# Attention block in fp32: maxima split and turned on VectorE, later q and k split on GpSimd

## The chip, the cores and the metric

The kernel runs on one core of a Trainium2 chip. The metric is device time in microseconds (us) of one execution, the median of several. Engines: TensorE (PE) for matrix products, VectorE (DVE), ScalarE (ACT), GpSimd (POOL), and SyncE (SP), which here only issues DMAs. They run side by side and meet at semaphores. Only PE writes products, to the memory PSUM; POOL and DMAs reach SBUF alone, not PSUM.

## What is computed

Eight batches of 512 rows of 128 numbers go through a layer norm with modulation, attention with 16 heads of 8 numbers, a gated sum, a second norm, and three dense layers with weights of +1 and -1. The attention, cut from the reference:

```python
pos = 1.0 + x * (1.0 + 0.5 * x * (1.0 + x / 3.0))
neg = 1.0 / (1.0 - x * (1.0 - 0.5 * x * (1.0 - x / 3.0)))
...
logits = logits - jnp.max(logits, axis=axis, keepdims=True)
s = _stablemax3_s(logits)
return s / jnp.sum(s, axis=axis, keepdims=True)
...
h = _layernorm(x, axis=-1) * (1 + ca) + sa
x = x + ga * _L0_attn_ref(h, L0_attn_w_qkv, L0_attn_w_out, L0_attn_b_out)
h = _layernorm(x, axis=-1) * (1 + cb) + sb
x = x + gb * _L0_ffn_ref(h, L0_ffn_k0, L0_ffn_k1, L0_ffn_k2, L0_ffn_s0, L0_ffn_s1, L0_ffn_s2)
```

After the maximum is taken off no logit is positive, so only the branch `neg` is used: one over a cubic.

## The kernel before, in words

The work is cut into 128 groups, 16 for each batch. A group m is two heads' worth of 512 x 256 scores, and belongs to a quad of four groups (`QUAD`). The program runs in steps s from -16 to 159; a block is 16 steps (b = s // 16, n = s % 16), and "step 5" below means n = 5. Every engine has its own function for a step (`pe_step`, `act_step`, `dve_step`, `pool_step`, `sp_step`), and each executes its instructions strictly in the order in which they are written there.

In step s the group s is finished and the logits of group s + 7 (`AHEAD`) are made, only for their row maxima:

- PE: `logits` writes the logits of two heads into the PSUM tensor SA (two banks, one for each head); `scores` writes scores, with the maximum taken off by two extra rows of the operand QH, into Z (two halves); `with_v` multiplies finished probabilities by v, five steps later; `misc` puts in pieces of the other layers at the places "a", "c" and "d" of the step, by the tables `MAIN` and `MISC`.
- ACT: `square_of` squares Z (L541), `prob_of` takes the reciprocal root of group s - 2 (L552), `take` copies products of the other layers out of PSUM.
- DVE: `cubic` (L701) twice and `maxima` (L712) twice, in turn. These four are the large DVE instructions. SA is a single buffer, so PE and DVE pass it to and fro.
- POOL: squares the cubic's result (L844), one instruction of 128x2048 per step, and norms (`normalise`, L850), gate products and copies.

A product in single precision is made of parts: a value is stored as a high part (rounded, type fp32r) and a low part (the rest). For q and k of the next batch, ACT writes the high part from PSUM (L568) and DVE the low part from PSUM (`split`, L734); SP writes both to memory (`write_parts`, L344) and reads them back spread over rows (`read_parts`, L348).

The maxima must go from a column for each row of q into rows of QH. Once in a quad, at n = 1, 5, 9 and 13: PE transposes the 128x16 maxima into SA's second bank (`maxima_across`, L484); DVE writes high and low part from there (`take_maxima`, L723 and L725); SP sends them to QH with four DMAs (L978). As the second bank of SA is taken for that time, the first logits of the next quad are made for each head alone (`alone`), and reduced in two instructions of 128x512. Behind these four DMAs SP issues the four that gather numerators and denominators of a finished quad (nd<-OT, L989). At n = 6 ACT squares the denominators of the whole batch (`den_sq`, L603), which needs all gathers.

MISC and AT say in which step and place the pieces of the other layers and of the norms stand; block 7 has no q, k and v to make, and blocks 8 and 9 hold what is left after the last group.

## Time and profile before

| | us |
|---|---|
| median of 3 runs | 790.41 (789.8 to 790.81) |
| the profiled execution | 786.48 |
| its span in the trace | 784.6 |
| steps 0 to 127 (47.4 to 724.6) | 677 |
| before the first cubic, after the last | 47, 60 |
| DVE busy in the span | 660.6 (84%) |
| PE, ACT, POOL busy | 654.2, 590.3, 584.9 |

Times in rows are microseconds from the start of the span, unless ns stands there. A name like mx<-SA is the tensor written and the one read. Idle time of an engine stands in brackets with the instruction that ended it. The clock of PE has two levels in this trace, 1.2 and 2.4 GHz: the column PEclk is its granted share, 1.00 for 2.4 GHz.

### The profile page before, as it was taken

To read this page: it belongs to the slowest core of one execution; us is meant where nothing else is said; L and a number is where in the kernel's file an instruction comes from. 1 tells how busy PE (TensorE), PEld (TensorE's weight loads), DVE (VectorE), ACT (ScalarE), POOL (GpSimd) and SP (SyncE) were. 2 spreads that over 40 slices of the span, in tenths; PEclk is the share of its full clock that TensorE was granted. 3 is DMA by queue.
4 is the path that set the end of the run, shared out by engine and by line. 5 is a ranking of instruction groups with operands and counts; after the bars stand their busy time and mean duration, and the time that the engine had idled before them with its cause. 6 is when DMAs were issued, how large, how long until landed. Compare 5 with 4: busy or idle time off the path is not lost.

```text
span 784.6 us, 9551 instructions
## 1 busy us (share of the span) xinstructions
PE 654.2 (83%) x2897; PEld 242.1 (31%) x2897; DVE 660.6 (84%) x806; ACT 590.3 (75%) x539; POOL 584.9 (75%) x348
## 2 busy tenths in 40 slices
...
DMA packets 41110, 56.35 MB, mean 72 GB/s; under 512 B 7852, under 2 KB 24516, under 8 KB 41060
## 3 DMA queue, kind: packets, MB, share of 16 engines
...
## 4 chain that ended last, share of the span: by engine, by line
PE 44%; DVE 24%; issue 15%; ACT 14%; DMA 1%; ACTq 0%; DVEq 0%; POOL 0%; POOLq 0%
DVE mx L712 12%; PE MB L417 10%; DVE cub L701 9%; PE OP L499 8%; PE SA L478 8%; PE Z L458 7%; ACT prob L552 5%; ACT sq L541 5%; PE MB L426 3%; PE SA L417 2%; PE MB L391 2%; ACT hid L582 2%; PE SA L426 1%; PE MB L394 1%; PE MB L410 1%
## 5 line engine op out<-in xcount | busy, mean ns | idle before, releaser
L844 POOL TENSOR_TENSOR cub<-cub 128x2048 f32<-128x2048 f32 x128 | 460.3, 3604 | 111.4 <-DVE cub L701 111.4
L541 ACT ACTIVATE sq<-Z,shift 128x1024 f32<-128x1024 f32 x256 | 282.9, 1117 | 110.9 <-PE Z L458 108.8
L712 DVE TENSOR_REDUCE mx<-SA 128x2 f32<-128x1024 f32 (+1 forms) x278 | 307.0, 1105 | 35.9 <-PE SA L478 34.6
L701 DVE SCALAR_TENSOR_TENSOR cub<-sq,Z 128x1024 f32<-128x1024 f32 x256 | 309.5, 1210 | 12.1 <-ACT sq L541 10.8
L552 ACT ACTIVATE prob<-cub 128x2048 f32<-128x2048 f32 x128 | 244.2, 1910 | 0.0
L478 PE MATMUL SA<-KH,QL 64*128 64x512 f32 x496 | 145.7, 523 | 62.3 <-DVE mx L712 51.4
L458 PE MATMUL Z<-QH,KH 64*128 64x512 f32 x512 | 139.8, 536 | 28.9 <-DVE cub L701 28.0
L499 PE MATMUL OP<-prob,Vq 128*16 128x512 f32 x1024 | 145.1, 641 | 1.4 <-ACT OT L590 1.4
L458 PEld LDWEIGHTS Z<-QH,KH 64*128 64x128 f32 x512 | 52.5, 199 | 222.3 <-DVE cub L701 145.7
L417 PE MATMUL MB<-hid,W 128*128 128x512 f32 x216 | 119.3, 640 | 0.0
L478 PEld LDWEIGHTS SA<-KH,QL 64*128 64x128 f32 x496 | 56.6, 200 | 162.0 <-DVE mx L712 132.1
L582 ACT ACTIVATE hid<-MB,sv 128x512 f32<-128x512 f32 x57 | 39.4, 691 | 9.1 <-PE MB L417 6.7
L410 PE MATMUL MB<-h2T,W 128*128 128x512 f32 x60 | 34.5, 658 | 9.5 <-ACT hid L582 7.8
L417 PEld LDWEIGHTS MB<-hid,W 128*128 128x128 f32 x216 | 32.9, 188 | 29.7 <-issue 28.8
L499 PEld LDWEIGHTS OP<-prob,Vq 128*16 128x16 f32 x1024 | 17.1, 95 | 38.6 <-issue 35.9
L426 PE MATMUL MB<-W2G,hid 128*128 128x128 f32 x192 | 27.3, 287 | 0.0
L753 DVE TENSOR_TENSOR y<-SA,x1k 128x512 f32<-128x512 f32 x2 | 1.4, 692 | 28.8 <-PE SA L426 28.8
L426 PEld LDWEIGHTS MB<-W2G,hid 128*128 128x128 f32 x192 | 23.1, 191 | 5.4 <-issue 5.4
L572 ACT ACTIVATE Vn<-MB 128x512 f32<-128x512 f32 x8 | 4.8, 600 | 24.4 <-PE MB L394 24.4
L814 POOL TENSOR_TENSOR rs<-mv,eps 128x4 f32<-128x4 f32 x16 | 3.3, 206 | 25.9 <-DVE mv L776 17.9
L850 POOL TENSOR_SCALAR x1n<-x,mv,rs 128x128 f32<-128x128 f32 x28 | 21.9, 800 | 0.7
L850 POOL TENSOR_SCALAR xn<-xa,mv,rs 128x128 f32<-128x128 f32 x28 | 21.9, 800 | 0.1
...
## 6 DMA issues: line engine op xcount, KB each, us to landing
...
nd<-OT SPq DMA_DIRECT2D x128, 32.0 KB
...
QH<-mp SPq DMA_DIRECT2D x128, 4.0 KB
```

The source lines that it names most:

```text
L417: mm = nc.tensor.matmul(bank, W1[:, kc, m * P:(m + 1) * P], hid[0][:, kc, :], start=(kc == 0), stop=(kc == KC - 1))
L426: mm = nc.tensor.matmul(bank4[:, t, :], hid[1][:, kc, t * P:(t + 1) * P], W2G[:, kc, :], start=(kc == 0), stop=(kc == KC - 1))
L458: mm = nc.tensor.matmul(Z[:, h, e * S:(e + 1) * S], KH[rows, 2 * g + r, keys], QH[rows, 2 * g + r, :], start=True, stop=True)
L478: nc.tensor.matmul(unit_bank(m, u)[:, e, :], QL[rows, 2 * g + r, qt * P:(qt + 1) * P], KH[rows, 2 * g + r, :], start=True, stop=True).then ...
L499: mm = nc.tensor.matmul(OP[32 * j:32 * j + 2 * HD, :], Vq[:, tb, hh, :, :].rearrange("p d a -> p (d a)"), slot[:, tb % 2, j % 2, :], start ...
L541: nc.scalar.activation(sq[:, h, :], Z[:, h, :], ACT.Square, bias=shift[:, 0:1]).then_inc(s_sq, 1)
L552: nc.scalar.activation(prob[:, m % RING, :], cub[:, m % RING].rearrange("p a n -> p (a n)"), RSQRT)\
L582: nc.scalar.activation(hid[layer][:, j, :], bank, ACT.Relu, scale=sv[:, layer:layer + 1])\
L701: nc.vector.scalar_tensor_tensor(cub[:, m % RING, h, :], sq[:, h, :], CUB_ADD, Z[:, h, :], ALU.add, ALU.mult).then_inc(s_cv, 1)
L712: nc.vector.tensor_reduce(to, unit_bank(m, u)[:, heads[0]:heads[-1] + 1, :], AX_X, ALU.max)\
L844: nc.gpsimd.tensor_tensor(ff, ff, ff, ALU.mult).then_inc(s_fp, 1)
L850: last = nc.gpsimd.tensor_scalar(dst[:, t, :], src[:, t, :], mv[:, t, 0:1], rs[:, t:t + 1], ALU.subtract, ALU.mult)
```

## The change

- The raw maxima (mx, 128x16 in SBUF) are first split into high and low part by DVE, in SBUF (`of_maxima`, stages 0 and 1), into ms (128x32); then DVE turns ms in blocks of 32x32 (stage 2, into mp). PE's transpose, its semaphore and `alone` are gone: the first logits of a quad are made and reduced like all others. The DMAs to QH are eight per quad (`M_DMAS`), one for each head and 32 partitions, in pieces of 128 bytes.
- From the second batch on, ACT copies q and k unsplit to SBUF, which frees the PSUM bank, and POOL makes both parts in SBUF (`parts_of`), at n = 1 and 2. SP waits for POOL's semaphores. k's product moves from place "d" of step 1 to "c", POOL's copy of v for quad 2 from step 1 to 3.
- `normalise` of POOL computes x * rs + nm with nm = -mean * rs in place of (x - mean) * rs; two instructions on 128x4 make nm.
- In the block ahead of the first group v is made at step 2. In block 7 x1, y and what follows move one step or a place ahead, and the second norm's statistics and root too; in block 8 l1_1 is cut into two halves (steps 0 and 1) and l1_2 is made in one piece in step 4.

```diff
-    ("hT", 1, [(0, "c", 4)]), ("q", 1, [(0, "d", 4)]), ("k", 1, [(1, "d", 4)]),
+    ("hT", 1, [(0, "c", 4)]), ("q", 1, [(0, "d", 4)]), ("k", 1, [(1, "c", 4)]),
...
+MISC[FIRST] = [("hT", 1, [(0, "c", 4)]), ("q", 1, [(0, "d", 4)]), ("k", 1, [(1, "d", 4)]), ("v", 1, [(2, "c", 4)])]
...
-    ("l1_1", -2, [(0, "c", 4)]), ("l1_2", -2, [(2, "c", 2), (4, "d", 2)]), ("l1_3", -2, [(5, "c", 4)]),
+    ("l1_1", -2, [(0, "c", 2), (1, "d", 2)]), ("l1_2", -2, [(4, "d", 4)]), ("l1_3", -2, [(5, "c", 4)]),
...
-AT[B - 1] = MAIN_AT | {"w2g": 4, "mv2": 9, "rs2": 10, "x1n": 10}
+AT[B - 1] = MAIN_AT | {"w2g": 4, "st2": 8, "mv2": 8, "rs2": 9, "x1n": 9}
...
-            def maxima_across(m):
-                if 0 <= m < GROUPS and m % QUAD == QUAD - 1:
-                    pe.wait_ge(s_mx, 4 * (m + 1))
-                    nc.tensor.transpose(SA[0:QUAD * TB, 1, 0:P], mx[:, m // QUAD % 2, :], ident[:, :]).then_inc(s_mt, 1)
...
-            if alone(m):
-                logits(m, 0, (1,))
             misc("a")
-            logits(m, 1, (0, 1))
+            logits(m, 1)
...
                             need(act, s_parts[name], beta * 4 * 16)
...
+                            if beta == 0:
+                                nc.scalar.activation(dst[:, 0, :], bank, ACT.Copy, scale=scale).then_inc(s_hi, 1)
+                            else:
+                                nc.scalar.activation(dst[:, 1, :].bitcast(F32), bank, ACT.Copy, scale=scale)\
+                                    .then_inc(s_taken[name], 1)
...
+                raw = mx[:, i, :].rearrange("p (e c) -> p e c", e=2)
+                if stage == 0:
+                    dve.wait_ge(s_mx, 2 * m)
+                    nc.vector.tensor_scalar(ms[:, i, :, 0, :], raw, -1.0, None, ALU.mult).then_inc(s_mh, 1)
+                elif stage == 1:
+                    dve.wait_ge(s_mh, quad + 1)
+                    nc.vector.scalar_tensor_tensor(ms[:, i, :, 1, :], raw, -1.0, ms[:, i, :, 0, :].bitcast(F32),
+                                                   ALU.mult, ALU.subtract).then_inc(s_ml, 1)
+                else:
+                    dve.wait_ge(s_ml, quad + 1)
+                    if quad >= 2:
+                        dve.wait_ge(s_mrow[(quad - 2) % NQ], ((quad - 2) // NQ + 1) * M_DMAS * 16)
+                    nc.vector.transpose(mp[:, i, :], ms[:, i].rearrange("p e a c -> p (e a c)").bitcast(F32))\
+                        .then_inc(s_mp, 1)
...
             cubic(s, 0)
-            take_maxima(m)
-            if alone(m):
-                maxima(m, 0, (0,))
-                maxima(m, 0, (1,))
-            else:
-                maxima(m, 0, (0, 1))
+            of_maxima(m, 0)
+            maxima(m, 0)
+            of_maxima(m, 1)
             split(b, n)
...
             cubic(s, 1)
-            maxima(m, 1, (0, 1))
+            of_maxima(m, 2)
+            maxima(m, 1)
...
+            def normalise(beta, k, src, mv, rs, nm, dst, s_rs, s_free, s_nm, s_done):
                 pool.wait_ge(s_rs, beta + 1)
+                nc.gpsimd.tensor_tensor(nm[:, :], mv[:, :, 0], rs[:, :], ALU.mult).then_inc(s_nm, 1)
+                pool.wait_ge(s_nm, 2 * k + 1)
+                nc.gpsimd.tensor_scalar(nm[:, :], nm[:, :], -1.0, 0.0, ALU.mult, ALU.add).then_inc(s_nm, 1)
+                pool.wait_ge(s_nm, 2 * k + 2)
                 need(pool, s_free, beta)
                 for t in range(TB):
-                    last = nc.gpsimd.tensor_scalar(dst[:, t, :], src[:, t, :], mv[:, t, 0:1], rs[:, t:t + 1],
-                                                   ALU.subtract, ALU.mult)
+                    last = nc.gpsimd.tensor_scalar(dst[:, t, :], src[:, t, :], rs[:, t:t + 1], nm[:, t:t + 1],
+                                                   ALU.mult, ALU.add)
...
+            def parts_of(beta, name):
+                if beta >= B:
+                    return
+                src = SQ if name == "q" else SK
+                i = 2 * beta + "qk".index(name)
+                pool.wait_ge(s_taken[name], beta + 1)
+                nc.gpsimd.tensor_scalar(src[:, 0, :], src[:, 1, :].bitcast(F32), 1.0, 0.0, ALU.mult, ALU.add)\
+                    .then_inc(s_hi, 1)
+                pool.wait_ge(s_hi, i + 1)
+                nc.gpsimd.tensor_tensor(src[:, 1, :], src[:, 1, :].bitcast(F32), src[:, 0, :].bitcast(F32), ALU.subtract)\
+                    .then_inc(s_lo, 1)
...
-            if n in (1, 5):
-                v_in(b, 2 if n == 1 else 3)
+            if n in (1, 2) and 0 <= b < B:
+                parts_of(b + 1, "qk"[n - 1])
+            if n in (3, 5):
+                v_in(b, 2 if n == 3 else 3)
...
                 for e in range(2):
-                    for a in range(PARTS):
-                        r = ROWS * e + R_MAX + a
-                        sp.dma_start(QH[r:r + 1, 2 * g:2 * g + 2, :].bitcast(F32), mp[2 * TB * e:2 * TB * (e + 1), quad % 2, a, :].bitcast(F32))\
+                    r = ROWS * e + R_MAX
+                    for k in range(P // 32):
+                        of = 32 * k + QUAD * TB * e
+                        sp.dma_start(rows_g[r:r + PARTS, :, :, k, :].bitcast(F32), mp[of:of + QUAD * TB, quad % 2, :])\
                             .then_inc(s_mrow[g], 16)
```

On DVE a step with a turn (n = 5 of block 0; the others are alike) is, before:

```order
L701 SCALAR_TENSOR_TENSOR cub<-sq,Z 128x1024
L723 TENSOR_SCALAR mp<-SA 16x128
L725 SCALAR_TENSOR_TENSOR mp<-SA,mp 16x128
L712 TENSOR_REDUCE mx<-SA 128x1 x2
L701 SCALAR_TENSOR_TENSOR cub<-sq,Z 128x1024
L712 TENSOR_REDUCE mx<-SA 128x2
```

and after:

```order
L699 SCALAR_TENSOR_TENSOR cub<-sq,Z 128x1024
L719 TENSOR_SCALAR ms<-mx 128x2x8
L708 TENSOR_REDUCE mx<-SA 128x2
L722 SCALAR_TENSOR_TENSOR ms<-mx,ms 128x2x8
L699 SCALAR_TENSOR_TENSOR cub<-sq,Z 128x1024
L728 STREAM_TRANSPOSE mp<-ms 128x32
L708 TENSOR_REDUCE mx<-SA 128x2
```

The two small instructions no longer stand together and no longer read SA; one stands on each side of the first reduction, which is whole again, and the transpose stands ahead of the second.

On SP the loads of a quad, the maxima (QH<-mp) and the gathers (nd<-OT) before:

```order
L348 DMA QL<-parts_q 32x1024 x2
L348 DMA KH<-parts_k 32x1024 x2
L348 DMA QH<-parts_q 32x1024 x2
L978 DMA QH<-mp 1x8x128 x4
L989 DMA nd<-OT 8x2x512 x4
```

and after:

```order
L354 DMA QL<-parts_q 32x1024 x2
L354 DMA KH<-parts_k 32x1024 x2
L354 DMA QH<-parts_q 32x1024 x2
L999 DMA QH<-mp 2x8x32 x8
L1010 DMA nd<-OT 8x2x512 x4
```

The order is the same; eight DMAs stand ahead of the gathers in place of four.

On POOL the steps 0 to 5 of a block (x1k is step 0's copy, cub<-cub a step's square), before:

```order
L865 TENSOR_SCALAR x1k<-x 128x512
L844 TENSOR_TENSOR cub<-cub 128x2048
L860 COPY Vq<-Vn 128x4x32
L844 TENSOR_TENSOR cub<-cub 128x2048 x4
L860 COPY Vq<-Vn 128x4x32
L873 TENSOR_TENSOR woG<-wo,gA 128x128
```

and after:

```order
L882 TENSOR_SCALAR x1k<-x 128x512
L845 TENSOR_TENSOR cub<-cub 128x2048
L865 TENSOR_SCALAR SQ<-SQ 128x512
L868 TENSOR_TENSOR SQ<-SQ 128x512
L845 TENSOR_TENSOR cub<-cub 128x2048
L865 TENSOR_SCALAR SK<-SK 128x512
L868 TENSOR_TENSOR SK<-SK 128x512
L845 TENSOR_TENSOR cub<-cub 128x2048
L877 COPY Vq<-Vn 128x4x32
L845 TENSOR_TENSOR cub<-cub 128x2048 x2
L877 COPY Vq<-Vn 128x4x32
L892 TENSOR_TENSOR woG<-wo,gA 128x128
```

The parts of q stand ahead of the square of step 1, those of k ahead of the square of step 2.

## Rows read from the trace of the kernel before

**Rows 1.** Windows: step 1 of block 1; block 3 and its steps 1, 2, 5, 9, 13.
```profile
core 0: us, PE busy (x) PEld busy (x) DVE busy (x) ACT busy (x) POOL busy (x), PEclk, DMA share, GB/s
136.35:145.58 9.23, 8.42 (x25) 2.73 (x25) 5.93 (x10) 5.75 (x6) 3.84 (x3) 0.50 0.07 17
306.16:391.76 85.60, 76.50 (x361) 27.70 (x361) 80.38 (x96) 73.30 (x68) 72.49 (x44) 1.00 0.27 81
311.20:318.54 7.34, 4.68 (x23) 1.52 (x21) 5.84 (x9) 5.90 (x7) 3.67 (x3) 1.00 0.05 13
318.54:324.38 5.84, 4.45 (x20) 1.47 (x20) 5.21 (x6) 4.40 (x5) 3.60 (x2) 1.00 0.81 297
333.71:339.71 6.00, 5.22 (x22) 1.66 (x22) 5.15 (x8) 4.40 (x5) 4.26 (x4) 1.00 0.03 8
354.64:361.19 6.55, 5.52 (x29) 2.23 (x28) 6.51 (x14) 5.47 (x6) 6.47 (x8) 1.00 0.04 9
375.38:382.06 6.68, 5.65 (x38) 3.22 (x38) 5.75 (x10) 4.69 (x5) 6.68 (x3) 1.00 0.04 11
```

**Rows 2.** Timeline of step 5, block 3: start us, us, engine line, what, [idle before].
```profile
332.74 3.60 POOL L844 TENSOR_TENSOR cub<-cub 128x2048 f32<-128x2048 f32 x1 [1.20 <-DVE cub L701]
333.71 1.21 DVE L701 SCALAR_TENSOR_TENSOR cub<-sq,Z 128x1024 f32<-128x1024 f32 x1
...
334.84 0.27 DVE L723 TENSOR_SCALAR mp<-SA 16x128 fp32r<-16x128 f32 x1
...
335.35 0.67 DVE L712 TENSOR_REDUCE mx<-SA 128x1 f32<-128x512 f32 x1
...
336.84 0.69 DVE L712 TENSOR_REDUCE mx<-SA 128x1 f32<-128x512 f32 x1 [0.82 <-PE SA L478]
...
338.58 1.22 DVE L712 TENSOR_REDUCE mx<-SA 128x2 f32<-128x1024 f32 x1
```

**Rows 3.** Groups by line: line engine op, shapes, count | busy us, mean ns | idle.
```profile
L850 POOL TENSOR_SCALAR xn<-xa,mv,rs 128x128 f32<-128x128 f32 x28 | 21.9, 800 | 0.1
...
L882 POOL TENSOR_TENSOR nd<-nd 128x512 f32<-128x512 f32 x7 | 8.9, 1276 | 14.0 <-ACT nd L596 14.0
...
L734 DVE SCALAR_TENSOR_TENSOR SQ<-MB,SQ 128x512 fp32r<-128x512 f32 x8 | 5.4, 680 | 0.9 <-ACT SQ L568 0.9
```

**Rows 4.** Timeline at start and end; L661 and L785: ns min/median/max.
```profile
5.32 1.03 POOL L816 TENSOR_TENSOR rs<-rs,half 128x4 f32<-128x4 f32 x1
...
5.99 0.28 DVE L637 TENSOR_TENSOR prob<-prob 8x128 f32<-8x128 f32 x1
...
9.26 1.90 POOL L832 TENSOR_SCALAR W<-prob 128x2048 f32<-128x2048 uint8 x1 [2.00 <-DMA prob<-L_ffn_k]
...
L661 DVE TENSOR_SCALAR mod<-mod x2: 158/580/1001, 10.2 to 11.1; 128x8 f32<-128x8 f32 x2
...
753.48 0.62 POOL L865 TENSOR_SCALAR x1k<-x 128x512 f32<-128x512 f32 x1 [1.61 <-DVE y L753]
...
L785 DVE TENSOR_SCALAR x1n<-x,mv,rs x4: 332/337/695, 753.2 to 754.4; 128x128 f32<-128x128 f32 x4
```

**Rows 5.** Timeline of SP's issues (SPq) and ACT, steps 5 to 8; landing of loads (L348).
```profile
335.45 2.79 SPq L978 DMA_DIRECT2D QH<-mp  x4
...
338.29 2.84 SPq L989 DMA_DIRECT2D nd<-OT  x4
...
345.38 0.62 ACT L603 ACTIVATE nd<-nd 128x512 f32<-128x512 f32 x1
...
347.70 1.10 ACT L541 ACTIVATE sq<-Z,shift 128x1024 f32<-128x1024 f32 x1
...
350.11 1.19 DVE L701 SCALAR_TENSOR_TENSOR cub<-sq,Z 128x1024 f32<-128x1024 f32 x1
...
DMA to landing us min/median/max: 2.0/2.7/4.8
```

**Rows 6.** Timeline: POOL in step 13 of block 3, and ACT in block 8.
```profile
375.45 7.17 POOL L844 TENSOR_TENSOR cub<-cub 128x2048 f32<-128x2048 f32 x2
...
731.32 0.69 ACT L582 ACTIVATE hid<-MB,sv 128x512 f32<-128x512 f32 x1 [3.91 <-PE MB L417]
```

More of the change, by code:

```diff
@@ L55 @@
 LOADS = 4
+M_DMAS = 8
 FIRST = -1
@@ L74 @@
 ]
-MISC = {b: MAIN for b in range(FIRST, B - 1)}
+MISC = {b: MAIN for b in range(B - 1)}
+MISC[FIRST] = [("hT", 1, [(0, "c", 4)]), ("q", 1, [(0, "d", 4)]), ("k", 1, [(1, "d", 4)]), ("v", 1, [(2, "c", 4)])]
 MISC[B - 1] = [
@@ L460, in scores, with logits @@
                 mm.then_inc(s_z, 1)
-            def logits(m, u, heads):
+            def logits(m, u):
                 if not 0 <= m < GROUPS:
@@ L465, in logits @@
                 beta, g, r, qt = logits_at(m, u)
[L466 to L484 removed]
+                if m == 0 and u == 0:
+                    pe.wait_ge(s_gate, 1)
+                if m % QUAD == 0 and u == 0:
+                    pe.wait_ge(s_qk[g], (beta + 1) * LOADS * 16)
+                need(pe, s_mx, unit_before(m, u))
+                for e in range(2):
+                    rows = slice(ROWS * e, ROWS * (e + 1))
+                    mm = nc.tensor.matmul(unit_bank(m, u)[:, e, :], QL[rows, 2 * g + r, qt * P:(qt + 1) * P],
+                                          KH[rows, 2 * g + r, :], start=True, stop=True)
+                mm.then_inc(s_a, 1)
             def with_v(s):
@@ L512, in pe_step @@
             misc("c")
-            maxima_across(m)
-            logits(m + 1, 0, (0,) if alone(m + 1) else (0, 1))
+            logits(m + 1, 0)
             misc("d")
@@ L567, in take @@
                             need(act, s_parts[name], beta * 4 * 16)
[L568 to L569 removed]
+                            scale = SCALE if name == "q" else 1.0
+                            if beta == 0:
[3 more added lines that the diff above has]
+                                    .then_inc(s_taken[name], 1)
                         elif name == "v":
```

68 lines of the change are left out of this document (24 added, 44 removed), and 12 rows, old and new, of the table MISC.

## The prediction

> **What bounds the kernel now.** I read the windows by stretch first: they show which engine fills a block and a step. A block (16 steps, one batch) takes 85.6 us at full clock; VectorE (DVE) is busy 80.4 of them, TensorE (PE) 76.5, ScalarE (ACT) 73.3, GpSimd (POOL) 72.5 [rows 1]. So DVE is the bound, with 5.2 us idle per block, and nobody has more than 13 us to spare. Then the timeline of step 5, to see what one step is made of: each of the four large DVE instructions starts 1.13 us after the one before it (333.71 to 334.84) [rows 2], so a bare step is 4 x 1.13 = 4.5 us and a bare block 72. The other 13 us are extras of DVE and waits. The steps in which four groups' maxima are turned (1, 5, 9, 13) take 7.3, 6.0, 6.55 and 6.7 us, and step 2, with the split of k, 5.8 [rows 1].
>
> **The change part by part** (per full block, against the profiled execution, 786.48 us, which is 3.93 below the median of 790.41; I add that at the end).
>
> 1. *The turn leaves TensorE and PSUM.* Step 5 now: two small instructions, two half-size reductions, and 0.8 us of DVE idle while PE makes the second head's logits (336.84 after 335.35 + 0.67) [rows 2]. Without them the step would be 4.5 plus three small instructions of 0.1 to 0.2 us, about 5.0: a gain of 1.0 in step 5. Step 9 holds x1's sum and statistics and has no idle, so it gains 0.3; step 13 gains 1.05.
>
> 2. *But the new instructions read SBUF, and POOL is at work there.* The first of them (ms<-mx) is a TENSOR_SCALAR from SBUF to SBUF. DVE has this form in two places next to a running POOL instruction. L661, on 8 elements, took 0.16 us once and 1.00 us the other time: it started at 10.2 and ended at 11.2, as POOL's L832 (9.26 + 1.90) ended at 11.16. L785 took 0.33 us, and 0.70 us where POOL's L865 ran (753.48 to 754.10) [rows 4]. So it is held until the POOL instruction in flight ends. In the loop of before no DVE instruction has this form; the old ones read PSUM. In step 5 the place of the new one is 334.84, and POOL's square (332.74 + 3.60) ends at 336.34: a hold of 1.5 us [rows 2]. This is no accident: the square starts when the last cubic ends, two pitches and 0.2 us earlier, so in each such step the hold is about 1.5 us, and more where POOL is behind. The step becomes 1.13 + 1.5 + 0.15 + 1.13 + 0.15 + 1.13 + 0.2 + 1.13 = 6.5 us in place of 6.0; I add 0.25 because POOL has new work just before it (part 3). **Step 5: +0.75.** Step 13: POOL is behind after the norms; its square of 375.45 + 3.60 ends 2.5 us after the place at 376.5 [rows 6]. With shorter norms I take a hold of 1.6 and y's sum: 7.3 against 6.7, **+0.6** (+3 if the norms stay long). Step 9: the first hold is 0.2, since POOL is then in the short W2G pieces. The second instruction (ms<-mx,ms) has two SBUF inputs and comes 1.3 us later, in a square. The one row of such an instruction beside POOL is L637, 0.28 us inside POOL's L816 (5.32 to 6.35), not held, but that one moves 4 elements [rows 4]. Bounds 0 and 3.6 (a whole square); I take 1.5, nearer to the row that was not held. **Step 9: +1.5.** The transpose has no row; I take 0.2 (bounds 0.1 and the 0.7 of a 512 column instruction [rows 3]) and no hold.
>
> The Trainium skill (SBUF — State Buffer, Who interferes with whom) says that DVE in a two-port mode and, with two SBUF inputs, against a reading POOL instruction, waits for the shared port for the whole instruction. For the first form the rows above agree; for the second no row here shows it. By that rule step 9 would cost up to 3.7 in place of 1.5.
>
> 3. *q and k.* DVE loses two splits (0.68 us, pitch 0.6 [rows 3]); POOL gains two copies of 0.62 (as L865 [rows 4]) and two subtractions of 1.28 (as L882 [rows 3]), 3.8 us per block in steps 1 and 2. Step 1: idle for the second head and the split go (1.5 + 0.6), the hold comes (square of step 0 ends 1.3 us after the place). Chain: hold to +2.45, small 0.15, reduction to 3.7, cubic to 5.0, transpose, reduction to 6.3. **Step 1: 6.3 for 7.3, -1.05.** Step 2: the bank is free after ACT's copy and k stands ahead of the logits; one wait of 0.3 is left: 4.85 for 5.85, **-1.0.** POOL's 3.8 us are hidden in its slack of 0.9 us per step by step 5, but for the 0.25 to 0.5 counted there. If POOL had no slack, they would cost up to 3.8.
>
> 4. *The queue of SyncE.* The turned maxima leave in 8 DMAs in place of 4, and about 4 us later in the step. One takes 0.70 us to issue (2.79 for 4, start to start 0.7), and behind them stand the 4 that gather numerators (2.84) [rows 5]. The last gather of a batch lands about 2.7 us after its issue, the median of the loads [rows 5], and ACT's square of the denominators in step 6 needs it. Before: last issue at 340.4, landed 343.1, used at 345.38: 2.3 us to spare. After: first maxima DMA at step + 5.8, last gather at 5.8 + 5.6 + 2.1 = 13.5, landed 16.1; natural time of the square 6.75 + 5.65 = 12.4. ACT stops for 3.7 us, and since the next ACT square (347.70 + 1.10) has only 1.3 us to the cubic that needs it (350.11) [rows 5], 2.4 go through. **Step 8: +2.4** (0 if a new DMA issues in 0.4 us as the loads do). The maxima themselves land at 5.8 + 4.9 + 2.7 = 13.4 after the step's start and are needed at about 13.6: just in time, which is a second way to lose up to 1 us four times a block.
>
> 5. *Norms.* 8 instructions of 0.80 [rows 3] become multiply-add. Nearest rows: 0.80 (same scalars from memory) and 0.62 for four times the elements (L865, multiply-add with constants), that is 0.2 to 0.8. I take 0.3, as the form differs from L865 only in where the scalars are; four new 4-element instructions cost 1.1 with their waits. POOL: 3.8 + 1.1 - 4.0 = +0.9 per block, off the path unless the norms stay at 0.80.
>
> 6. *Start and end.* v early and the first two turns without PE: -2.5 (POOL has no squares yet). Tail: ACT waits 3.9 us for l1_1 ahead of two probabilities [rows 6]; with l1_1 cut in two this goes, but PE's remaining products then end it: -1.5, and -1 for block 7's order.
>
> Sum per full block: -1.05 - 1.0 + 0.75 + 2.4 + 1.5 + 0.6 = +3.2. Blocks 2 to 6: +16. Block 1, in part at half clock: its step 1 of 9.2 us [rows 1] gets 2.2 shorter, its steps 5 and 13, short before, get 1.6 longer each, the rest as above: +2.4. Block 0 (no gathers yet): -0.3. Block 7 (no q, k): +3.2. Start and end: -5. Together +16: 786.5 + 16 + 3.9 = **806 us**.
>
> **Rivals.**
> - *No hold* (the two old rows have another cause). Then steps 1, 2, 5, 9, 13 give 1.9 + 0.9 + 1.0 + 0.3 + 1.05 = 5.15 and the queue takes 2.2 back: -2.95 in five blocks, -11 in blocks 0, 1 and 7, -5 outside: -31, **759 us**; 745 if the queue costs nothing too. For it: the new instructions have 16 elements. Against it: L661 had 8. Chance 0.20.
> - *Hold, but the queue costs nothing*: new DMAs issue like the loads (0.42) or land sooner. +16 - 7 x 2.4 = -1: **790 us**, no change that can be measured, or just off it. Chance 0.12.
> - *Hold and long norms*: 0.80 stays, POOL falls 4 us further behind, step 13 costs 3.7 and step 9 more; also the clock may fall to 1.2 GHz where holds thin PE out, as in block 1. +3 to +4 per block more: **up to 828**. It is inside the forecast's chance of 0.68.
> - The change does what it says: the order shows each new instruction in its place.
>
> **How the numbers follow.** Forecast 0.68 (794 to 828), no hold 0.20 (740 to 772), no queue cost 0.12 (785 to 796). 0.2% is 1.6 us, about what a measurement of this kernel can tell. Slower: 0.68 + 0.03; the same: 0.06; faster: 0.20 + 0.03. From 766 to 828 it leaves out some 0.13 below and 0.06 above; the forecast's own range is 794 to 828.
>
> **What the profile after would show.** If right: ms<-mx with a mean near 1.5 us, ended as POOL's square ends; ACT idle before nd<-nd (den_sq) for 3 to 4 us in each block; steps 1 and 2 shorter by 1 us each. If wrong: ms<-mx at 0.1 to 0.2 us with POOL busy beside it, and step 5 near 5.0. If norms stay at 0.80, step 13 is above 8.

## The result: 4.4% slower, more than twice the forecast loss

| | before | after |
|---|---|---|
| median, us | 790.1 (786.4 to 790.8, 4 runs) | 825.0 (820.4 to 827.1, 4 runs) |
| the profiled execution | 786.48 | 826.7 |
| its span, and mean granted PE clock | 784.6, 0.915 | 824.9, 0.875 |

The ratio is 1.044, interval 1.039 to 1.050. The forecast was 806: the direction and the range held, the size did not. It said +16; the medians say +35, and the two profiled executions, against which the sum was made, +40. Medians here and below are of all executions; the ratios and their intervals leave out those more than 1.5% above the fastest of the same kernel.

The page of the kernel after, first line, clock by slices (the span in 40 parts, tenths of full speed), and shares of the chain that ended last, by line:

```profile
span 824.9 us, 9372 instructions
...
PEclk9555777857799899988999899998999989979999
...
DVE cub L699 11%; DVE mx L708 10%; ACT sq L535 7%; PE MB L423 6%; PE OP L496 6%; ACT prob L546 5%; DVE ms L719 5%; SPq L999 5%; PE SA L479 4%; PE Z L464 4%; PE SA L423 2%; DMA nd<-OT 2%; DVE ms L722 2%; SPq L1010 2%; ACT hid L580 2%
```

All suspects are in the chain: the first split L719 (5%), the second L722 (2%), the queue L999 and L1010 (7%), and the gathers' landing. Windows of the kernel after, to hold against [rows 1]: block 3, its steps 1, 2, 5, 7, 9, 10 and 13, then step 10 of block 6, where the clock was full (stretch, length, busy time of each engine with its count, PEclk, DMA share, GB/s):

```profile
core 0: us, PE busy (x) PEld busy (x) DVE busy (x) ACT busy (x) POOL busy (x), PEclk, DMA share, GB/s
317.87:408.30 90.43, 79.54 (x357) 28.95 (x357) 83.18 (x94) 73.31 (x68) 74.14 (x52) 0.92 0.26 77
322.91:328.79 5.88, 4.69 (x23) 1.66 (x22) 5.88 (x7) 5.79 (x7) 3.63 (x3) 1.00 0.27 69
328.79:333.33 4.54, 3.72 (x19) 1.16 (x18) 4.54 (x5) 4.27 (x5) 4.54 (x3) 1.00 0.02 3
342.77:349.35 6.58, 5.05 (x21) 1.48 (x21) 6.58 (x8) 4.58 (x5) 4.78 (x4) 1.00 0.39 122
354.67:361.77 7.10, 6.43 (x25) 1.95 (x24) 4.88 (x9) 3.63 (x5) 2.43 (x1) 1.00 0.47 129
366.68:376.08 9.40, 7.22 (x32) 3.67 (x28) 7.12 (x12) 5.45 (x6) 8.73 (x9) 0.68 0.00 0
376.08:382.24 6.16, 6.16 (x21) 1.74 (x20) 4.97 (x10) 3.01 (x4) 5.88 (x8) 0.64 0.06 14
391.86:398.71 6.85, 5.45 (x38) 3.24 (x38) 6.85 (x10) 4.83 (x5) 3.81 (x2) 1.00 0.00 1
...
649.77:654.58 4.81, 4.10 (x20) 1.28 (x18) 4.81 (x10) 3.18 (x3) 3.02 (x2) 1.00 0.02 3
```

Steps 1 and 2 are shorter by 1.5 and 1.3 us. Steps 5, 7, 9 and 10 are longer, by 0.6, 2.3, 2.9 and 1.4 (steps 7 and 10 took 4.8 before). And the clock, 1.00 in all of block 3 before, is 0.92 here, with its lows in steps 9 and 10.

**The hold.** The instructions that work on ms (count, ns min/median/max, first and last start):

```profile
L719 DVE TENSOR_SCALAR ms<-mx x32: 167/1528/3327, 37.0 to 738.3; 128x16 fp32r<-128x16 f32 x32
L722 DVE SCALAR_TENSOR_TENSOR ms<-mx,ms x32: 157/159/3344, 38.3 to 738.5; 128x16 fp32r<-128x16 f32 x32
L728 DVE STREAM_TRANSPOSE mp<-ms x32: 195/198/211, 38.5 to 739.8; 128x32 f32<-128x32 f32 x32
```

The same instruction takes 0.17 or 3.33 us, so it is not its work that takes the time. POOL of the kernel after around step 5 of block 3 and VectorE in it (start, us), to hold against [rows 2]:

```profile
342.23 3.60 POOL L845 TENSOR_TENSOR cub<-cub 128x2048 f32<-128x2048 f32 x1
...
343.90 1.96 DVE L719 TENSOR_SCALAR ms<-mx 128x16 fp32r<-128x16 f32 x1
...
346.91 0.16 DVE L722 SCALAR_TENSOR_TENSOR ms<-mx,ms 128x16 fp32r<-128x16 f32 x1
```

POOL's square ends at 345.83, L719 at 345.86. So it goes throughout: of the 31 times that L719 began with a POOL instruction in flight, it ended 28 to 35 ns after that instruction 30 times. Step 9 of block 4 is the worst case, and it falls on the second instruction:

```profile
458.21 0.22 DVE L719 TENSOR_SCALAR ms<-mx 128x16 fp32r<-128x16 f32 x1
459.20 3.59 POOL L845 TENSOR_TENSOR cub<-cub 128x2048 f32<-128x2048 f32 x1
459.49 3.34 DVE L722 SCALAR_TENSOR_TENSOR ms<-mx,ms 128x16 fp32r<-128x16 f32 x1
```

The square had begun 0.29 us before, and L722 ends 0.04 after it (462.83 and 462.79). Blocks 2 and 5 show the same 3.34 us. In blocks 3 and 6 VectorE had first waited 2.3 and 2.1 us for PE's logits (PE was at 1.2 GHz), L722 came later and was held for 0.97 and 1.20; it was again released as POOL's square ended, and step 9 lasts 9.4 us in all five blocks. Only one POOL instruction held nothing: L817, a root of 128x4.

```profile
737.68 1.02 POOL L817 TENSOR_TENSOR rs<-rs,half 128x4 f32<-128x4 f32 x1
738.34 0.17 DVE L719 TENSOR_SCALAR ms<-mx 128x16 fp32r<-128x16 f32 x1
```

**The queue.** SP's issues after step 5 of block 3, ACT's square of the denominators with its idle time, the next ACT square that a cubic needs, and that cubic; then who waited, in the whole run. To hold against [rows 5]:

```profile
348.35 5.35 SPq L999 DMA_DIRECT2D QH<-mp  x8
353.75 2.84 SPq L1010 DMA_DIRECT2D nd<-OT  x4
...
358.31 0.63 ACT L601 ACTIVATE nd<-nd 128x512 f32<-128x512 f32 x1 [3.47 <-DMA nd<-OT]
...
360.64 1.10 ACT L535 ACTIVATE sq<-Z,shift 128x1024 f32<-128x1024 f32 x1
...
361.77 1.22 DVE L699 SCALAR_TENSOR_TENSOR cub<-sq,Z 128x1024 f32<-128x1024 f32 x1 [2.23 <-ACT sq L535]
...
ACT nd L601: 20.9, 7
```

The last gather is issued 13.1 us after the step's start (forecast 13.5), ACT goes on at 15.5 (16.1), it stood for 3.5 (3.7), and 2.2 go through to the cubic (2.4).

**Where the 40 us are.** I worked these out from the starts of the cubics in the two profiled executions.

| | forecast, us | measured, us |
|---|---|---|
| blocks 2 to 6 | +16 | +28.9 (85.7 to 91.5 a block) |
| block 1 | +2.4 | +4.0 |
| block 0 | -0.3 | +1.7 |
| block 7 | +3.2, and -1 for its order | +10.0 |
| before the first cubic | -2.5 | 0.0 |
| after the last cubic | -1.5 | -4.3 |

So 13 us are missing in the full blocks and 8 in block 7. The small differences of blocks 0 and 1 can't be read: the kernel before ran between 784.4 and 794.4 us in the comparisons below, and its block 0 and that of kernels with the same start and turn take 84.0 to 87.7 us, with the clock low for 57 to 74 of them. The experiments were made to put a name to the rest.

### The profile page after: what moved, and what is told of

Its sections match the earlier page's. It is cut to its first block, busy times and chain, and to the rows that moved or that the text cites. A ratio compares the mean times of both kernels' runs of the same rounds, so it can differ in the third digit from the quotient of the medians.

```text
span 824.9 us, 9372 instructions
## 1 busy us (share of the span) xinstructions
PE 663.4 (80%) x2865; PEld 244.6 (30%) x2865; DVE 694.8 (84%) x794; ACT 590.5 (72%) x539; POOL 596.7 (72%) x404
## 4 chain that ended last, share of the span: by engine, by line
DVE 30%; PE 29%; issue 15%; ACT 15%; SPq 7%; DMA 3%; ACTq 0%; POOL 0%; DVEq 0%; POOLq 0%
DVE cub L699 11%; DVE mx L708 10%; ACT sq L535 7%; PE MB L423 6%; PE OP L496 6%; ACT prob L546 5%; DVE ms L719 5%; SPq L999 5%; PE SA L479 4%; PE Z L464 4%; PE SA L423 2%; DMA nd<-OT 2%; DVE ms L722 2%; SPq L1010 2%; ACT hid L580 2%
## 5 line engine op out<-in xcount | busy, mean ns | idle before, releaser
L708 DVE TENSOR_REDUCE mx<-SA 128x2 f32<-128x1024 f32 x248 | 301.2, 1214 | 38.9 <-PE SA L479 36.0
L479 PE MATMUL SA<-KH,QL 64*128 64x512 f32 x496 | 135.9, 544 | 77.0 <-DVE mx L708 67.0
L464 PE MATMUL Z<-QH,KH 64*128 64x512 f32 x512 | 141.8, 550 | 45.5 <-DVE cub L699 41.0
L496 PE MATMUL OP<-prob,Vq 128*16 128x512 f32 x1024 | 153.6, 678 | 0.4 <-ACT OT L588 0.4
L423 PE MATMUL MB<-hid,W 128*128 128x512 f32 x216 | 127.6, 680 | 0.3 <-ACT hid L580 0.3
L479 PEld LDWEIGHTS SA<-KH,QL 64*128 64x128 f32 x496 | 52.8, 209 | 174.3 <-DVE mx L708 131.6
L719 DVE TENSOR_SCALAR ms<-mx 128x16 fp32r<-128x16 f32 x32 | 46.9, 1465 | 0.0
L901 POOL TENSOR_TENSOR nd<-nd 128x512 f32<-128x512 f32 x7 | 8.9, 1277 | 35.7 <-ACT nd L594 35.7
L588 ACT ACTIVATE OT<-OP 128x512 f32<-128x512 f32 x32 | 19.2, 600 | 1.7 <-PE OP L496 1.7
L601 ACT ACTIVATE nd<-nd 128x512 f32<-128x512 f32 x8 | 5.0, 629 | 20.9 <-DMA nd<-OT 20.9
```

Of the source, the lines that this page charges most:

```text
L423: mm = nc.tensor.matmul(bank, W1[:, kc, m * P:(m + 1) * P], hid[0][:, kc, :], start=(kc == 0), stop=(kc == KC - 1))
L464: mm = nc.tensor.matmul(Z[:, h, e * S:(e + 1) * S], KH[rows, 2 * g + r, keys], QH[rows, 2 * g + r, :], start=True, stop=True)
L479: mm = nc.tensor.matmul(unit_bank(m, u)[:, e, :], QL[rows, 2 * g + r, qt * P:(qt + 1) * P], KH[rows, 2 * g + r, :], start=True, stop=True)
L496: mm = nc.tensor.matmul(OP[32 * j:32 * j + 2 * HD, :], Vq[:, tb, hh, :, :].rearrange("p d a -> p (d a)"), slot[:, tb % 2, j % 2, :], start ...
L708: nc.vector.tensor_reduce(to, unit_bank(m, u)[:, :, :], AX_X, ALU.max).then_inc(s_mx, 1)
L719: nc.vector.tensor_scalar(ms[:, i, :, 0, :], raw, -1.0, None, ALU.mult).then_inc(s_mh, 1)
```

## The experiments

Each ran beside the kernel before on the same chip; its median there stands beside each. "A full block" is the mean of blocks 2 to 6: 85.7 us before, 91.5 after.

### Taking the hold away by the form of the instruction

```diff
-                    nc.vector.tensor_scalar(ms[:, i, :, 0, :], raw, -1.0, None, ALU.mult).then_inc(s_mh, 1)
+                    nc.vector.tensor_reduce(ms[:, i, 0, :, 0, :], raw, AX_X, ALU.max, negate=True).then_inc(s_mh, 1)
...
-                    nc.vector.scalar_tensor_tensor(ms[:, i, :, 1, :], raw, -1.0, ms[:, i, :, 0, :].bitcast(F32),
-                                                   ALU.mult, ALU.subtract).then_inc(s_ml, 1)
...
+                    nc.vector.tensor_reduce(ms[:, i, 0, :, 1, :], both, AX_X, ALU.add, negate=True).then_inc(s_ml, 1)
```

(The raw maxima lie in the same tensor ms, so that `both` is raw maximum and high part side by side.)

> The changed kernel with both splits of the maxima written as TENSOR_REDUCE with negation (high part: the largest of one element, negated; low part: the sum of the raw maximum and the high part, negated). Place, sizes and results stay. Theory (the two instructions are held while a POOL instruction runs, and the PE clock falls because PE starves behind the held DVE): both splits take 0.15 to 0.2 us each in place of 1.47 and 0.52 us on the mean; step 1 falls from 5.9 to about 4.9 us, step 5 from 6.6 to 5.1, step 9 from 9.4 to 6.3, step 13 from 7.3 to 5.7, and steps 6, 10 and 14 lose 0.2 to 0.8 each with the low clock gone: -8 per full block, about 768 us (760 to 780). Rival (POOL is close enough to the bound that it takes the place): the splits get short but half of the gain comes back as waits for POOL's square: about 795. Rival (the hold has nothing to do with the form of the instruction): TENSOR_REDUCE is held as well, 825.

Measured: 771.0 us (before 786.5; ratio 0.976, 0.969 to 0.984). The two splits of this kernel, and its block 3:

```profile
L719 DVE TENSOR_REDUCE ms<-ms x32: 160/163/170, 37.5 to 680.9; 128x16 fp32r<-128x16 f32 x32
L723 DVE TENSOR_REDUCE ms<-ms x32: 175/177/186, 38.7 to 681.1; 128x16 fp32r<-128x32 f32 x32
...
294.51:379.04 84.53, 76.54 (x357) 28.12 (x357) 78.02 (x95) 73.16 (x68) 74.00 (x52) 0.96 0.28 82
```

At the same places, over the same data and beside the same POOL instructions nothing is held any more: L719 began with up to 3.37 us of a POOL instruction left and never took more than 0.17. The expectation was 768 us; step 1 kept 5.5 us where 4.9 was expected. A full block falls from 91.5 to 83.6: the hold with all that follows from it costs 7.9 us per block. The rival with POOL as the next bound is out.

### The queue of SyncE

The block of code that issues the four gathers stands ahead of the one that issues the eight maxima DMAs; nothing else differs:

```diff
...
+                    sp.dma_start(nd[r:r + HD, :, :], OT[32 * j:32 * j + 2 * HD, quad % 2, :]).then_inc(s_gat[quad % 2], 16)
+
             if (s + AHEAD - 4) % QUAD == 0 and 0 <= s + AHEAD - 4 < GROUPS:
```

> The changed kernel with SyncE issuing the four gathers of numerators and denominators ahead of the eight maxima DMAs; nothing else. Theory (queue): the last gather of a batch lands early again, ACT's square of the denominators no longer waits (20.9 us in total in the changed kernel, under 1 here), and step 7, 7.0 us on the mean against 4.8 before the change, goes back to about 4.8: -2.2 in seven blocks, about 810 us. Rival (step 7 is long because of the hold in step 5 and the statistics, and the wait of ACT lies beside them): the wait goes, the time stays within 3 us of 825. The maxima DMAs are not later, since the gathers' data are ready 4 us before the turned maxima.

Measured: 806.1 us (before 786.5; ratio 1.023, 1.017 to 1.029). ACT's wait for nd<-OT is gone from the list of waits, step 7 is back at 4.8, and a full block falls by 3.9 us. That is more than the 2.2 expected, and the largest part of the surplus is in step 9, which falls from 9.4 to 8.7. The late denominators also make POOL's product late (its idle time before nd<-nd was 35.7 us in the kernel after, 14.0 in this one as before [rows 3]), and with it all that POOL does next. So the square that holds L722 in step 9 starts 2.1 us after the step's start in the kernel after (block 4) and 1.2 here, and L722 is held for 3.34 us there and 2.38 here:

```profile
444.81 3.60 POOL L845 TENSOR_TENSOR cub<-cub 128x2048 f32<-128x2048 f32 x1
446.06 2.38 DVE L722 SCALAR_TENSOR_TENSOR ms<-mx,ms 128x16 fp32r<-128x16 f32 x1
```

Without the hold the late product costs step 9 nothing by itself. In the kernel of the first experiment, where the gathers are late and nothing is held, step 9 is 8.60 us in block 3 and 6.18 in block 5. POOL's product begins 13.0 and 13.1 us after the start of step 6 in both; what differs is the clock:

```profile
341.21:349.81 8.60, 7.29 (x34) 3.55 (x30) 6.26 (x12) 5.72 (x6) 8.52 (x9) 0.78 0.00 0
509.20:515.38 6.18, 4.80 (x25) 1.69 (x23) 6.18 (x13) 5.59 (x6) 6.10 (x8) 1.00 0.00 0
```

> Both edits in one: splits as TENSOR_REDUCE, and gathers ahead of the maxima DMAs. Theory: the two costs are separate, so the gains add: -57 and -15 from 825, about 753 us, which is also 37 below the kernel before. Rival (one cost hides behind the other, or the eight maxima DMAs then land too late for PE): 765 to 780, with PE waiting for them at the start of a quad.

Measured: 747.1 us (before 786.5; ratio 0.946, 0.939 to 0.953). This kernel has both edits. Its block 3 and step 9:

```profile
288.82:368.35 79.53, 73.80 (x357) 26.96 (x357) 77.83 (x94) 73.15 (x68) 73.92 (x52) 1.00 0.30 87
...
332.84:339.14 6.30, 5.12 (x28) 2.03 (x27) 6.26 (x14) 5.55 (x6) 6.22 (x8) 1.00 0.09 21
```

The two costs add: with the other one gone, the hold is worth 8.2 (87.6 to 79.4) and the queue 4.2 (83.6 to 79.4). Of these 4.2 only 2.7 are paid at full clock: block 5 of the kernel with only the hold gone had no low clock and took 82.2. In blocks 2 to 6 of the kernel with both edits the clock is 1.00 throughout. What is left of the change gains 6.3 us per full block against the kernel before.

### The hold by itself, in the kernel before

One instruction of 16 elements, 32 times, whose result is not used, at the place where the kernel after has L719:

```diff
+                dve.wait_ge(s_mx, 4 * m)
+                nc.vector.tensor_scalar(md[:, :], mx[:, i, :], -1.0, None, ALU.mult)
                 dve.wait_ge(s_mt, quad + 1)
```

> The kernel before, with one more instruction per quad on VectorE at the place where the changed kernel has ms<-mx: TENSOR_SCALAR, 128x16, SBUF to SBUF, its result is not used. This is the disputed cost by itself, 32 times. Theory (held until POOL's square ends, and the PE clock falls behind it): about 1.5 us each in steps 1 and 5, 2.3 in step 13, 0.3 in step 9; steps 1, 5 and 13 get 1.6 to 2.4 longer, and steps 5 to 14 of the later blocks show stretches at 1.2 GHz as the changed kernel's do (7 to 14 us per block): +40 on 786, about 826 us. Rival (a hold of DVE costs only its own length, the clock falls for another reason of the changed kernel): +30, 816, and no low clock in blocks 2 to 7.

The control has `nc.vector.tensor_reduce(md[:, :], mx[:, i, :].unsqueeze(2), AX_X, ALU.max, negate=True)` there.

> The same as the extra TENSOR_SCALAR, at the same place and size, but as TENSOR_REDUCE (maximum of one element, negated), the form that was not held in the changed kernel. Theory: 0.16 us each, with its wait 0.3 us per quad: +8, about 794 us, clock as in the kernel before. Rival (any instruction put there delays PE's turn enough to thin PE out): clock low in the later blocks, over 800.

Measured: 821.6 us for the first (before 787.7; ratio 1.041, 1.036 to 1.046), 789.2 for the control (1.000, 0.996 to 1.003). The instruction in the one, in step 13 of block 3 with POOL's squares, the windows of steps 13 and 14; and the instruction in the control:

```profile
L722 DVE TENSOR_SCALAR md<-mx x32: 166/1511/3515, 36.7 to 728.4; 128x16 f32<-128x16 f32 x32
...
389.97 7.16 POOL L847 TENSOR_TENSOR cub<-cub 128x2048 f32<-128x2048 f32 x2
391.16 2.44 DVE L722 TENSOR_SCALAR md<-mx 128x16 f32<-128x16 f32 x1
...
390.03:398.16 8.13, 6.16 (x33) 2.82 (x32) 8.10 (x10) 4.25 (x4) 8.06 (x3) 0.84 0.01 2
398.16:404.08 5.92, 5.58 (x31) 2.74 (x32) 4.70 (x5) 5.21 (x6) 4.01 (x3) 0.93 0.52 114
```

```profile
L722 DVE TENSOR_REDUCE md<-mx x32: 157/160/170, 37.2 to 701.9; 128x16 f32<-128x16 f32 x32
```

The first of the two squares ends at 393.57 (389.97 + 3.60), the instruction at 393.60. So 16 elements at the wrong moment cost this kernel 4%, as much as the whole change. Two more things are to be read. Step 1 takes 7.34 us with and without the extra instruction, since VectorE stood for 1.5 us there anyway (7.34 less 5.84 busy [rows 1]): a hold costs only what no wait covers (step 5, held for 1.53, gets 0.6 longer; step 13, held for 2.4 to 3.5, 1.75). And step 14, which has no such instruction, is 6.2 on the mean of blocks 2 to 6 against 4.8: after the hold of 2.4 in step 13 the granted clock is 0.84 in step 13 and 0.93 in step 14. In the control it is 1.00 in both (6.68 and 4.73 us). The expectation missed that the lows are confined to the longest hold: 3 to 7 us per block in and behind step 13, not 7 to 14.

### Place and form

The kernel after with both splits in their old form, but 1.2 us later (behind the first reduction, ahead of the second cubic):

```diff
             cubic(s, 0)
-            of_maxima(m, 0)
             maxima(m, 0)
-            of_maxima(m, 1)
...
+            of_maxima(m, 0)
+            of_maxima(m, 1)
             cubic(s, 1)
```

> The changed kernel with both splits in their old form, but placed after the first reduction of the step, just ahead of the second cubic (1.2 us later for the first one). Theory (the hold lasts to the end of the POOL instruction in flight, so the place alone sets it): the first hold falls from 1.5 to about 0.3 us in steps 1, 5 and 13; in step 9 POOL has by then begun its square, so one of the two is held for 2 to 3 us as before; steps 1, 5, 13 lose 1.0 to 1.3 each, step 9 nothing: -4 to -5 per block, about 790 us. Rival (the hold is a fixed price of the form and not of what POOL does at the moment): 825.

Measured: 801.0 us (before 787.7; ratio 1.016, 1.010 to 1.021). Its first split (the second takes 174 to 197 ns), and step 9 of block 3:

```profile
L719 DVE TENSOR_SCALAR ms<-mx x32: 160/267/2883, 38.3 to 711.3; 128x16 fp32r<-128x16 f32 x32
...
357.92 3.59 POOL L845 TENSOR_TENSOR cub<-cub 128x2048 f32<-128x2048 f32 x1
358.66 2.88 DVE L719 TENSOR_SCALAR ms<-mx 128x16 fp32r<-128x16 f32 x1
```

The median of L719 falls from 1.53 to 0.27 and step 13 from 7.3 to 6.0; step 9 stays at 9.0, as expected. The place decides, not a fixed price. The time missed its expectation of 790 by 11: steps 1 and 5 gained 0.4 and 0.6 where 1.0 to 1.3 each was expected, and the low clock behind step 9 stayed. Now only the low part in its old form (two SBUF inputs), the rest as in the kernel with both edits:

```diff
-                        nc.vector.tensor_reduce(ms[:, i, 0, :, 1, :], both, AX_X, ALU.add, negate=True).then_inc(s_ml, 1)
+                    nc.vector.scalar_tensor_tensor(ms[:, i, 0, :, 1, :], ms[:, i, 1, :, 0, :].bitcast(F32), -1.0,
+                                                   ms[:, i, 0, :, 0, :].bitcast(F32), ALU.mult,
+                                                   ALU.subtract).then_inc(s_ml, 1)
```

> Gathers first, high part as TENSOR_REDUCE, but the low part again as the changed kernel has it: SCALAR_TENSOR_TENSOR with two SBUF inputs. This is the cost of the second instruction alone, which the prediction bounded by 0 and 3.6 in step 9. Theory (it is held until the POOL instruction in flight ends, as the first one is): in the kernel with both splits as TENSOR_REDUCE, POOL's square of step 9 starts 1.3 us ahead of this place, so it is held for some 2.3 us in step 9 and up to 0.9 where POOL is in the copy of q in step 1; elsewhere the square has ended: step 9 goes from 6.3 to 8.6, 747 + 7 x 2.4 = about 764 us. Rival (two SBUF inputs are not held, the long ones of the changed kernel have another cause): 747.

Measured: 775.1 us (before 789.5; ratio 0.982, 0.976 to 0.988). The low part, and step 9 of block 3:

```profile
L721 DVE SCALAR_TENSOR_TENSOR ms<-ms x32: 165/654/3033, 38.3 to 685.5; 128x16 fp32r<-128x16 f32 x32
...
344.63 3.60 POOL L845 TENSOR_TENSOR cub<-cub 128x2048 f32<-128x2048 f32 x1
345.88 2.38 DVE L721 SCALAR_TENSOR_TENSOR ms<-ms 128x16 fp32r<-128x16 f32 x1
```

It is held like the first one. Against the kernel with both edits step 9 goes from 6.3 to 8.6 (expected 8.6), but the whole costs 28 us in place of 17: steps 5 and 13 get 0.9 and 0.6 longer, and steps 10 and 11, which hold nothing of it, 0.85 and 0.6, with the clock at 0.84 in step 9. Again the clock was left out of the expectation.

### The rest of the change

The kernel after with the turn of the maxima as before: PE's transpose, `alone`, splits from PSUM and four DMAs are back.

```diff
-                rows_g = QH[:, 2 * g:2 * g + 2, :].rearrange("p r (t k i) -> p r t k i", t=TB, k=P // 32)
...
+            maxima_across(m)
+            logits(m + 1, 0, (0,) if alone(m + 1) else (0, 1))
```

> The changed kernel with the turn of the maxima as in the kernel before (PE transposes into PSUM, VectorE splits from there, four DMAs, first logits of a quad head by head); q and k by POOL, norms as multiply-add, the start and the end as changed. Theory (the loss is all in the turn): step 2 keeps its gain of 1.4 us (4.6), step 1 loses the split of q (6.7 for 7.3), no low clock in blocks 2 to 7, ends a little shorter: 790 - 6 x 2 - 4 = about 774 us. Rival (the work moved to POOL, or the moved pieces, cost by themselves): 790 or more, with waits of DVE for POOL or a low clock in the later blocks.

Measured: 776.0 us (before 786.5; ratio 0.985, 0.979 to 0.991). A full block is 84.4 (step 1 6.5, step 2 4.8 in block 3). But block 7 is 79.7 against 75.6, with the clock at 1.00: the new order of its pieces costs 4 us. The end after the last cubic is 55.6 us against 60.0. Where block 7 loses is seen best in the kernel with both edits, step 8 of block 7, VectorE:

```profile
649.58 1.23 DVE L707 TENSOR_REDUCE ms<-SA 128x2 f32<-128x1024 f32 x1 [1.46 <-PE SA L478]
650.73 0.68 DVE L752 TENSOR_TENSOR x<-MB,xb 128x512 f32<-128x512 f32 x1
```

x1's product stands in place "a", ahead of the logits on PE, and it waits for ACT to empty the bank; the reduction waits behind. Step 8 lasts 8.2 us, 3.4 more than before; 1.9 of it are x1's sum and statistics, which the old order has in step 9. So I put block 7's order back, with both edits kept:

```diff
-    ("x1", -1, [(8, "a", 4)]),
-    ("y", -2, [(9, "a", 1), (9, "c", 1), (9, "d", 1), (10, "a", 1)]),
+    ("x1", -1, [(8, "c", 4)]),
+    ("y", -2, [(9, "c", 1), (9, "d", 1), (10, "c", 1), (10, "d", 1)]),
...
-AT[B - 1] = MAIN_AT | {"w2g": 4, "st2": 8, "mv2": 8, "rs2": 9, "x1n": 9}
+AT[B - 1] = MAIN_AT | {"w2g": 4, "mv2": 9, "rs2": 10, "x1n": 10}
```

> Splits as TENSOR_REDUCE and gathers first, and the order of the other layers' pieces in block 7 as in the kernel before the change (x1, y and what follows one step or place later). Theory (the new order stops DVE: step 8 of block 7 takes 8.2 us against 4.8, and step 10 8.0 against 3.5): block 7 falls from 82.2 to about 73 us, the end after the last cubic grows from 57.4 to about 60: 747 - 7 = about 740 us. Rival (the stops of block 7 are the eight layers' own work, which then moves into the end): 745 to 748.

Measured: 740.2 us (before 787.7; ratio 0.938, 0.932 to 0.945). Block 7 of this kernel (its step 8 is 4.7):

```profile
605.45:678.76 73.31, 66.45 (x316) 23.07 (x315) 61.32 (x69) 70.10 (x64) 65.33 (x37) 1.00 0.10 26
```

Block 7 falls from 82.2 to 73.3, and the end grows from 57.4 to 58.8. This is the change without its three faults: 6% faster than the kernel before, and 10% faster than the kernel after.

Three parts alone, each added to the kernel before. Norms as multiply-add (`tensor_scalar(dst, src, rs, nm, ALU.mult, ALU.add)`):

> The kernel before, with only POOL's norms as multiply-add (and their two new small instructions). Theory: 0.45 us each for 0.80, POOL's work falls by 2.8 less 0.8 = 2 us per block, which lies off the path: the time stays within 2 us of 787. Rival (POOL's norms do push the square and the probabilities of steps 10 to 13): 780.

Measured: 790.2 us (before 789.5; ratio 1.000, 0.997 to 1.004): off the path. The split of q and k by POOL (`parts_of` and what belongs to it):

> The kernel before, with only the split of q and k by POOL in SBUF (the copy by ACT, v for quad 2 in step 3, k's product one place earlier). Theory (as the kernel with the old turn shows it): step 1 6.5 for 7.3 and step 2 5.4 for 6.0, nothing in the other steps: -1.5 in six blocks, about 778 us. Rival (POOL with the norms still long falls behind by its 3.8 us and gives back part of it in steps 3 to 5): 784.

Measured: 778.5 us, the median of four from 767.4 to 783.1 (before 789.5; ratio 0.979, 0.970 to 0.987, that is 10 to 24 us less). Step 1 is 6.5 us; the two blocks at full clock, 2 and 3, take 84.0 and 83.9 against 85.6. Start, block 7 and end (the tables `MISC` and `AT`):

> The kernel before, with only the start (v early), block 7's order of the other layers' pieces and the two halves of l1_1 in the end. Theory: the first cubic up to 1 us earlier, block 7 4 us longer (stops in steps 8 and 10), the end after the last cubic 4 us shorter: the time stays within 2 us of 787. Rival (the prediction's: start 2.5, block 7 1.0 and end 1.5 us less): 782.

Measured: 793.9 us (before 789.5; ratio 1.004, 1.000 to 1.008): no gain, at best; the forecast was -5. Its first cubic starts at 46.3 us, against 47.4 in the kernel before. Its block 7 takes 9.8 us more than before where 4 were expected. Here it is beside block 7 of the kernel with the old turn and the same order (the first line), which stayed at full clock:

```profile
638.53:718.27 79.74, 70.68 (x327) 24.53 (x330) 62.31 (x68) 70.20 (x64) 65.49 (x37) 1.00 0.06 17
...
655.18:740.56 85.38, 76.45 (x327) 26.69 (x330) 62.38 (x68) 70.75 (x64) 66.54 (x35) 0.92 0.06 16
```

The second trace is of an execution of 799.7 us, the longest of ten. But the kernel with both edits shows the same: block 7 of 82.2 us, clock 0.92.

## Why the forecast was right in direction and wrong in size

The sum for a full block was +3.2: -5.15 for a turn without a hold and the split on POOL, +5.95 for the hold, +2.4 for the queue. It came out as +5.8: -6.3, +8.2 and +3.9. What was too small in the last two is, for the larger part, one thing that the sum put at nothing: PE's clock (point 3).

1. **The turn without a hold** (forecast -5.15 per full block for steps 1, 2, 5, 9 and 13): the kernel with both edits shows -6.3, of which -5.8 in these five steps. Step 5 is 4.9 where 5.0 was forecast, step 1 5.5 where 5.4 follows from the forecast, step 9 6.3 (6.25), step 13 5.5 (5.6), step 2 4.5 (4.95). Right, step by step.

2. **The hold itself** (forecast 1.5 us, step 5 +0.75, step 13 +0.6, step 9 +1.5): right in steps 5 (+0.6) and 13 (+0.6 on the mean). The mean of L719 is 1.47 us. In step 9 the second instruction (L722) is held to the end of a whole square, 3.34 us in three of five blocks, not 1.5, and the step got 2.9 us longer: of the bounds 0 and 3.6 the truth was near the upper one. I had chosen by L637, the nearest row, which was not held [rows 4]. I misread it: it moves 128 elements on 8 partitions, not 4, and what sets it apart is the POOL instruction beside it, the root rs<-rs,half on 4 elements. That one did not hold L719 or L722 either (0.16 to 0.18 us four times beside L817), so the row said nothing about a square. The trace before had two more rows of the first form that I passed over, L641 (the first of four, 0.95 us from 6.38) and L668 (1.12 us from 17.67), each held until a MEMSET of POOL had ended (7.26 and 18.64). The rule of the Trainium skill (SBUF — State Buffer, Who interferes with whom) that speaks of two SBUF inputs against a POOL instruction that reads gave up to 3.7 for step 9; the runs agree with it, 3.34 us for L722 and 2.38 for the low part alone, but for the root just named, which held nothing. The same section says that on this chip TENSOR_REDUCE never contends; 160 to 186 ns in the kernel with both splits in that form agree.

3. **What the waits do to the clock: the term that failed.** The sum had nothing for it; I named it in a rival and gave it no price. Of the 7.9 us per block that the hold costs, 5.6 fall in the four steps with the new instructions, 1, 5, 9 and 13 (forecast 5.95). The other 2.3, or 11.5 us in five blocks, are the net of the other steps, in the main 6, 10, 11, 14 and 15, which contain none of them: step 10 takes 5.67 us on the mean against 4.80 without the hold, step 14 5.33 against 4.64, step 11 5.03 against 4.50. That these are the clock's shows inside the kernel after. Step 9 lasts 9.4 us in every block, but in block 6 the clock is full in steps 10 and 11 and they take 4.8 and 4.5; in block 3, where it is low in step 10, they take 6.2 and 4.9, in block 2 6.3 and 6.0. Step 14 takes 4.6 in blocks 2 and 3 at full clock and 5.7 to 5.9 in blocks 4 to 6. While VectorE is held, PE has little to do (its MATMULs waited up to 3.9 us for mx), and behind that, as behind ACT's wait for the gathers, the granted clock falls to 1.2 GHz: for 10 to 14 us of each of the blocks 2 to 7 (in block 3 the share is 0.92, and twice 0.08 of 90.4 us are 14); before, only block 4 had any (3.4). The price is seen in the eight products of a step with v, 1.91 us at the low level and 1.05 at the high one:

```profile
364.91 1.91 PE L496 MATMUL OP<-prob,Vq 128*16 128x512 f32 x8
...
372.02 1.05 PE L496 MATMUL OP<-prob,Vq 128*16 128x512 f32 x8
```

That the hold is the cause, and not some other part of the change, is shown by the pair in the kernel before: the held form has low clock behind step 13 in each block, the form that isn't held has none in blocks 2 to 5 (block 6 has 6.8 us in other steps, as in other kernels without a hold). Not each hold does it: behind 1.35 and 1.53 us in steps 1 and 5 the clock stayed full.

4. **The queue** (forecast +2.4 per block in step 8): measured 3.9 to 4.2. Issue times, landing and the part that goes through to the cubic were right within 0.6 us (it shows in step 7 by my borders, +2.2, and +0.35 in step 8). What failed is that "2.4 go through" was the whole. At full clock the queue costs 2.7 (82.2 against 79.5 in block 5), so the path was right. The rest depends on what stands beside it. With nothing held, ACT's wait thins PE out and the clock falls (0.96 in block 3 with only the hold gone): step 9 is 7.6 on the mean, 6.2 in the one block at full clock. With the hold, POOL's product is 3.6 us late, its square in step 9 0.9 later in the step, and so is the end of the hold. The second way to lose that I named, maxima that land too late for PE, hardly happened: one wait of 4.4 us in the whole run.

5. **Steps 1 and 2, q and k on POOL** (-1.05 and -1.0): they gave -1.45 each on the mean, 0.4 more than forecast. The part alone shortens step 1 by 0.9 and a full block at full clock by 1.7, with POOL's work hidden, and the kernel by 10 to 24 us.

6. **Norms**: 0.45 us, where I took 0.3 between 0.2 and 0.8; the new small ones 0.20 each. Off the path both in the forecast and by the part alone:

```profile
L855 POOL TENSOR_SCALAR xn<-xa,rs,nm 128x128 f32<-128x128 f32 x28 | 12.2, 448 | 0.7
```

7. **Start and end** (-5): wrong. The end gave 4.3, more than the 1.5 forecast. The start gave 0: with v early and the old turn the first cubic is at 46.3 and 46.4 us (46.8 to 47.7 in the kernels with v late), with the new turn at 46.9 to 47.9; which instruction takes it back I did not test. Block 7's order, forecast at -1, costs 4 us at full clock, and 8.9 (82.2 against 73.3) and 9.8 (85.4 against 75.6) where the clock fell to 0.92, with the new turn and with the old one. I had priced it by the order of the pieces alone and not looked at what stands on PE behind a piece that waits for its bank, nor at the clock behind that wait.

8. **Two sums.** The forecast for block 1 says +2.4, but its own terms (-2.2 + 3.2 - 1.0 + 2.4 + 1.5) make 3.9; measured 4.0. Block 7 was given the +3.2 of a full block, though it has no q and k to gain by. Right sums would have added some 3 us to the forecast, of the 19 that are missing.

Of the rivals, "no hold" and "the queue costs nothing" are out. "Up to 828" came nearest, but for half of its reason: the norms got short, it was the clock.

What stays open: the 1 us of the start; which wait makes the clock fall, since nearly the same hold in step 5 of the kernel after left it full in blocks 2 and 3 (1.96 us) and not in block 4 (1.97); and why block 7 with the old turn stayed at full clock in one kernel and not in the other.
